# Summing a block's edges in the expert stage: one product of 195 columns and a reduction on VectorE in place of three products of 65

## The chip, the core and the metric

The kernel runs on one core of a Trainium2 chip. The metric is the device time of one execution in microseconds; lower is better. The five engines that the text names are TensorE (PE in the rows, its weight loads PEld), VectorE (DVE), ScalarE (ACT), GpSimd (POOL) and SyncE (SP).

## What is computed

Two graph layers over 6250 nodes with 256 features. The part that matters here is the first graph convolution and the mixture of eight experts that follows it:

```python
# first layer, graph part
x = features * norm_src @ W_gcn            # 64 columns a node
agg = segment_sum(x[src], dst)             # 106250 edges
h = relu(agg * norm_dst + b_gcn) @ W_out + b_out
# then, on the normalised sum of x, h and an attention term
w = softmax(feat @ Wr + br)                # 8 experts
y = relu(bn(feat @ W1[e] + b1)); y = relu(bn(y @ W2[e] + b2)); y = y @ Wo[e] + bo
x = x + sum_e w[e] * y[e]
```

A second attention layer on the same graph and a second mixture with a router graph follow; the change does not touch them.

## The kernel before

**Edges.** Edges are sorted by destination and cut into blocks of 128 that each belong to one window of 128 nodes. Four blocks (GROUP) make a group. For each block GpSimd gathers 128 rows of a table in DRAM by an indirect DMA (line 1455). A row holds the 64 features and a one (65 columns, GCOL) as three bfloat16 parts (PARTS) that add up to the float32 value, 195 columns in a row. VectorE builds a one-hot matrix of the four blocks' destinations (`one_hot`, line 1776). TensorE multiplies it with the rows (`edges`, lines 1470 to 1480): for each block three products of 65 columns add up in one region of PSUM. VectorE then adds each block's 65 columns to its window's sums in SBUF (`add_edges`, line 1791), each addition waiting for the one before, as two blocks can have the same window.

**Buffers.** `pe` has two PSUM banks, one for even and one for odd groups. Before group q TensorE waits until group q-2 has been added (line 1475). There are five buffers of gathered rows (ROWS) and three one-hot matrices (HOTS); both come free by the count of multiplied groups, `s_sum`.

**The expert stage.** The 49 windows go through in 7 chunks of 7 windows, and each chunk goes through 8 experts: 56 units (c, e). Within a unit TensorE, in a fixed order written out by hand, does the second layer of the expert in four quarters (`layer`, line 1566, l = 1), the first layer of the next expert (l = 0), and the last layer in four pairs of windows (`last`, line 1579). VectorE takes each last product, weighs it with the gate and adds it to the result (`weighted`, line 1895). ScalarE applies the activation after each layer (line 1704). The units' other work on VectorE is a piece of the router's sort (`sort.vector`, lines 1170 to 1232), in five of the eight experts of each chunk (e = 1 to 5). Experts 0, 6 and 7 have little or no sorting; 6 and 7 prepare the next chunk.

**Where edges lie in a unit.** 187 groups are spread over units 0 to 45, mostly four in a unit, in chunk 0 five or six. `share(unit, k)` names the groups of quarter k. On TensorE they come: share 0 ahead of `layer` l = 1, share 1 behind it, share 2 behind the next expert's `layer` l = 0, share 3 between the second and the third `last`. On VectorE: share 0 first, then the sort's piece 0, share 1, piece 1, share 2, piece 2, two `weighted`, piece 3 (line 1963), share 3 (line 1956), two `weighted`. Ahead of each group VectorE loads four window numbers into registers. Every engine takes its instructions in order, so an instruction that waits holds up all that stand behind it on its engine.

Of the kernel before, what the change touches and what calls it, by code (L numbers as in the profile page):

```python
# [10 lines left out]
ALU = mybir.AluOpType  # L11
ACT = mybir.ActivationFunctionType
AXX = mybir.AxisListType.X
ENG = mybir.EngineType

P = 128
# [15 lines left out]
PARTS = 3  # L32
GCOL = GCN + 1
# [18 lines left out]
GROUP = 4  # L52
# [206 lines left out]
class Prelude:  # L259
# [6 lines left out]
    ROWS = 6  # L266
    HOTS = 3
    KCB = 3
# [3 lines left out]
    VCOL = P + 1  # L272
    PAIRS = HALFKV // P
    KROW = HALFKV + PAIRS * VCOL

# [10 lines left out]
    def __init__(self, f, nc, R, A):  # L286
# [12 lines left out]
        self.rows = f.sb("rows", [P, self.ROWS, GROUP, GPAD], BF16)  # L299
        self.hot = f.sb("hot", [P, self.HOTS, P, GROUP], BF16)  # L300
        self.count = f.sb("count", [P, P, GROUP], BF16)
# [81 lines left out]
    def tensor(self, t):  # L383
        R = self.R

        def edges(q):
# [5 lines left out]
            for u in range(GROUP):  # L392
                for k in range(PARTS):
                    mm = t.matmul(self.pe[:, q % 2, u * GCOL:(u + 1) * GCOL], self.hot[:, q % self.HOTS, :, u],
                                  self.rows[:, b, u, k * GCOL:(k + 1) * GCOL], start=(k == 0), stop=(k == PARTS - 1))
# [65 lines left out]
    def vector(self, v):  # L461
# [4 lines left out]
        def one_hot(q):  # L466
            if q >= self.GROUPS:
                return
            if q >= self.HOTS:
                v.wait_ge(self.s_sum, q - self.HOTS + 1)  # L470
            v.tensor_tensor(self.hot[:, q % self.HOTS], self.count[:, :, :],
                            R.gdst[:, GROUP * q:GROUP * (q + 1)].unsqueeze(1).to_broadcast([P, P, GROUP]),
# [73 lines left out]
class Front:  # L546
# [3 lines left out]
    HALVES = GB // BAT  # L550
# [694 lines left out]
class Stage1:  # L1245
# [7 lines left out]

    ROWS = 5
    HOTS = 3
    PAIRS = -(-TPI // 2)
    UNITS = ITER * E0

# [68 lines left out]
    def __init__(self, f, nc, R, A):  # L1327
        self.nc, self.R, self.A = nc, R, A
        self.GROUPS = self.need(ITER - 1)
        self.acc = R.gacc  # L1330
        PAIRS = self.PAIRS
        store = R.XT[:, :, :].rearrange("p c n -> p (c n)")
        size = E0 * C * D

        def weights(k):
            return store[:, k * size:(k + 1) * size].rearrange("p (e c d) -> p e c d", e=E0, c=C)

        self.w1, self.w2, self.wo = (weights(k) for k in range(3))
        self.mw2 = R.ahead.mw2
        self.wout = R.ahead.wout  # L1340
        self.b2 = R.ahead.b2
        self.bg = R.ahead.bg
        self.wr = R.ahead.wr
        self.br = R.ahead.br
        self.bo, self.bop = R.ahead.bo, R.ahead.bop
        self.gs = f.sb("gs", [P, TPI, PARTS * 32])
        self.gb = f.sb("gb", [P, TPI, E0], BF16)
        self.bn = R.ahead.bn
        self.scale = f.sb("scale", [P, 2, E0 * C])
        self.shift = f.sb("shift", [P, 2, E0 * C])  # L1350
        self.rows = f.sb("rows", [P, self.ROWS, GROUP, GPAD], BF16)
        self.hot = f.sb("hot", [P, self.HOTS, P, GROUP], BF16)
        self.count = f.sb("count", [P, P, GROUP], BF16)
        self.xm = R.ahead.xm
        self.hid = f.sb("hid", [P, C, TOK])
        self.hf = f.sb("hf", [P, TPI, GCOL])
        self.nd = f.sb("nd", [P, TPI])
        self.ht = f.sb("ht", [GCOL, TPI, P])
        self.stats = f.sb("stats", [P, TPI, 6])
        self.mv = f.sb("mv", [P, TPI, 2])  # L1360
        self.var = f.sb("var", [P, TPI])
        self.std = f.sb("std", [P, TPI])
        self.rstd = f.sb("rstd", [P, TPI])
        self.xn = f.sb("xn", [P, TPI, D])
        self.xt = f.sb("xt", [P, C, TOK])
        self.lg = f.sb("lg", [P, TPI, E0])
        self.mx = f.sb("mx", [P, TPI])
        self.gate = f.sb("gate", [P, 2, TPI, E0])
        self.gt = f.sb("gt", [PARTS * 32, TPI, P], BF16)
        self.h1 = f.sb("h1", [P, C, TOK])  # L1370
        self.h2 = f.sb("h2", [P, C, TOK])
        self.pe = f.ps("pe", [P, 2, 512])
        self.ph = f.ps("ph", [P, 3, 512])
        self.po = f.ps("po", [P, 2, 2, D])
        self.side = f.ps("side", [P, 512])
        self.s_w = [f.sem(f"w{e}") for e in range(E0)]
        self.s_st, self.s_bn, self.s_bnr, self.s_scaled, self.s_made, self.s_cnt = (
            f.sem(n) for n in ("st", "bn", "bnr", "scaled", "made", "cnt"))
        self.s_rows = [f.sem(f"rows{b}") for b in range(self.ROWS)]
        self.s_hot, self.s_sum, self.s_acc = (f.sem(n) for n in ("hot", "sum", "acc"))  # L1380
        self.s_xm, self.s_mixed, self.s_side, self.s_sa, self.s_x = (
            f.sem(n) for n in ("xm", "mixed", "side", "sa", "x"))
        self.s_hf, self.s_nd, self.s_ndr, self.s_hr = (f.sem(n) for n in ("hf", "nd", "ndr", "hr"))
        self.s_bs, self.s_mv, self.s_var, self.s_std, self.s_xn = (f.sem(n) for n in ("bs", "mv", "var", "std", "xn"))
        self.s_lr, self.s_lg, self.s_ex, self.s_gate, self.s_total = (
            f.sem(n) for n in ("lr", "lg", "ex", "gate", "total"))
        self.s_h, self.s_g, self.s_o, self.s_a = (f.sem(n) for n in ("h", "g", "o", "a"))
        self.sort = RouterSort(f, nc, R, A)
        self.at = {u: k for k, u in enumerate(self.uses())}
        self.free, acts = [], 0  # L1390
        for what, n, k in self.uses():
            if what == "y":
                self.free.append((self.s_x, 2 * TPI * n + min(2 * k + 2, TPI)))
            elif what == "bo":
                self.free.append((self.s_x, 2 * TPI * n + TPI + min(2 * k + 2, TPI)))
            elif what == "lg":
                self.free.append((self.s_lr, n + 1))
            elif what == "sum":
                self.free.append((self.s_total, 1))
            else:  # L1400
                acts += 1
                self.free.append((self.s_sa, acts))
# [44 lines left out]
    def pool(self, g):  # L1447
        self.sort.pool(g)
        for q in range(self.GROUPS):
            b = q % self.ROWS  # L1450
            if q >= self.ROWS:
                g.wait_ge(self.s_sum, q - self.ROWS + 1)
            for u in range(GROUP):
                t = GROUP * (self.first() + q) + u
                g.indirect_dma_start(self.rows[:, b, u, :], None, self.R.tab0,  # L1455
                                     bass.IndirectOffsetOnAxis(self.R.gsrc[:, t:t + 1], 0)).then_inc(self.s_rows[b], 16)
# [3 lines left out]
    def tensor(self, t):  # L1460
# [9 lines left out]
        def edges(q):  # L1470
            b = q % self.ROWS
            t.wait_ge(self.s_hot, q + 1)
            t.wait_ge(self.s_rows[b], 16 * GROUP * (q // self.ROWS + 1))
            if q >= 2:
                t.wait_ge(self.s_acc, GROUP * (q - 1))
            for u in range(GROUP):
                for k in range(PARTS):
                    mm = t.matmul(self.pe[:, q % 2, u * GCOL:(u + 1) * GCOL], self.hot[:, q % self.HOTS, :, u],  # L1478
                                  self.rows[:, b, u, k * GCOL:(k + 1) * GCOL], start=(k == 0), stop=(k == PARTS - 1))
            mm.then_inc(self.s_sum, 1)  # L1480

        def mix(n, q):
            take("mix", n, q)
# [271 lines left out]
    def vector(self, v):  # L1755
# [13 lines left out]
        def one_hot(q):  # L1769
            if q >= self.GROUPS:  # L1770
                return
            if q >= self.HOTS:
                v.wait_ge(self.s_sum, q - self.HOTS + 1)
            t = GROUP * (self.first() + q)
            dst = R.gdst[:, t:t + GROUP]
            v.tensor_tensor(self.hot[:, q % self.HOTS], self.count[:, :, :],
                            dst.unsqueeze(1).to_broadcast([P, P, GROUP]), ALU.is_equal).then_inc(self.s_hot, 1)

        def add_edges(qs):
            for q in qs:  # L1780
                t = GROUP * (self.first() + q)
                _, ws = self.nc.values_load_multi_w_load_instructions(
                    R.gwin[0:1, t:t + GROUP], engines=(ENG.DVE,), min_val=0, max_val=W - 1,
                    skip_runtime_bounds_check_because="a count of at most W - 1 windows")
                aws = placed(v, columns_of(self.acc, ws))
                one_hot(q + self.HOTS - 1)
                v.wait_ge(self.s_sum, q + 1)
                for u, aw in enumerate(aws):
                    if GROUP * q + u:
                        v.wait_ge(self.s_acc, GROUP * q + u)  # L1790
                    v.tensor_tensor(aw, aw, self.pe[:, q % 2, u * GCOL:(u + 1) * GCOL], ALU.add).then_inc(self.s_acc, 1)  # L1791

        def gather_sums(n, done):
            win[n] = self.windows(ENG.DVE, n)
# [1850 lines left out]
```

## Time and profile before

| | us |
|---|---|
| median of 3 runs | 4489.13 (4483.42 to 4490.09) |
| profiled execution | 4484.99 |
| its span | 4483.3 |
| TensorE busy | 3576.9 (80%) |
| VectorE busy | 3140.5 (70%) |
| GpSimd busy | 2788.0 (62%) |
| ScalarE busy | 2405.0 (54%) |

The span is the time from the first to the last instruction of the profiled execution; the execution's own time is a little longer. A share of busy time over the whole span averages stages with different limits, so a stage is read from windows of its own. The last edge products of this stage start at 1567.91 us.

### The profile page before, as it was taken

The page shows a single profiled execution, that of the slowest core. Times are in us where ns is not written, and L with a number is a line of the kernel's source. Part 1 is how long each engine was busy: PE and PEld are TensorE (multiplying, and loading weights), DVE is VectorE, ACT ScalarE, POOL GpSimd, SP SyncE. Part 2 cuts the span into 40 slices and gives each one's busy share as a digit, 9 for nine tenths or more (in the row PEclk, how much of TensorE's full clock was granted, in tenths as well). Part 3 has the DMA queues.
Part 4 walks back from the last instruction along what each step waited for, and adds up shares of the span by engine and source line. Part 5 has one row for each costly group of instructions (what it writes and reads, how often), then busy time and mean ns, then how long its engine had stood idle before and what let it go on. Part 6 is the DMA issues. An engine that isn't in the chain of part 4 may idle for free. (4 is left out here: it accounts for less than half of the span.)

```text
span 4483.3 us, 67252 instructions
## 1 busy us (share of the span) xinstructions
PE 3576.9 (80%) x17779; PEld 2293.6 (51%) x17779; DVE 3140.5 (70%) x10032; ACT 2405.0 (54%) x5559; POOL 2788.0 (62%) x2880
## 2 busy tenths in 40 slices
PE   6697889999999998678878778855277777777763
PEld 6654556666666665444444445534144444444442
DVE  7676566565655654788888888875567777777777
ACT  7243223333233333489999974434466666666664
POOL 0175577676665400377777777764777777777774
PEclk9998999999999999899999999975589989898986
DMA  3233122121221101555555555534222222222221
GB/s 100 69 95 107 38 48 47 34 46 34 44 43 30 31 1 37 158 138 145 144 143 142 143 151 161 159 94 117 33 40 40 40 39 41 39 40 39 40 39 28
DMA packets 291737, 331.29 MB, mean 74 GB/s; under 512 B 80182, under 2 KB 246062, under 8 KB 291366
## 3 DMA queue, kind: packets, MB, share of 16 engines
q0 software_dynamic: 105328, 175.77, 19.2%
q1 hardware_dynamic: 186038, 151.23, 12.4%
q8 instruction: 153, 2.51, 0.2%
q14 instruction: 218, 1.79, 0.1%
HBM read 289.56 MB, written 30.77 MB: 71 GB/s over the span
## 5 line engine op out<-in xcount | busy, mean ns | idle before, releaser
L3108 POOL DMA_INDIRECT st_rows<-tabr,router_rsrc x1072 | 1030.3, 961 | 329.8 <-issue 317.0
L2438 POOL DMA_INDIRECT all_XT<-tab,graph_gsrc x880 | 843.7, 959 | 268.1 <-issue 233.3
L1455 POOL DMA_INDIRECT st_rows<-tab,graph_gsrc x748 | 733.1, 980 | 393.2 <-issue 205.1
L1704 ACT ACTIVATE st_h<-st_ph,st_shift,st_scale 128x448 f32<-128x448 f32 x448 | 323.9, 723 | 744.6 <-PE st_ph L1566 744.3
L2468 PE MATMUL st_po<-all_XT,st_hot 128*128 128x264 f32 x1760 | 517.7, 441 | 108.2 <-DVE gat_sum L2678 105.4
L3165 PE MATMUL st_py<-st_w,st_hid 128*128 128x256 f32 x1568 | 440.9, 430 | 2.8 <-ACT st_hid L3213 2.8
L2468 PEld LDWEIGHTS st_po<-all_XT,st_hot 128*128 128x128 f32 x1760 | 300.3, 202 | 249.1 <-issue 114.3
L2678 DVE TENSOR_TENSOR gat_sum<-gat_sum,st_po 128x264 f32 x880 | 375.8, 427 | 70.9 <-PE st_po L2468 1.7
L3153 PE MATMUL st_px<-all_XT,st_w 128*128 128x512 f32 (+2 forms) x832 | 390.8, 616 | 14.8 <-ACT st_hid L3213 14.8
L3127 PE MATMUL st_pad<-st_adr,st_hott 128*128 x1072 | 68.0, 175 | 405.5 <-DVE st_zd L3279 393.0
L1579 PE MATMUL st_po<-all_XT,st_h 128*128 128x256 f32 x1568 | 371.0, 385 | 8.5 <-DVE all_X L1895 6.7
L1566 PE MATMUL st_ph<-st_xt,all_XT 128*128 128x448 f32 x896 | 357.0, 550 | 0.0
L1566 PE MATMUL st_ph<-st_h,all_XT 128*128 128x448 f32 x896 | 355.8, 544 | 0.0
L3165 PEld LDWEIGHTS st_py<-st_w,st_hid 128*128 128x128 f32 x1568 | 315.8, 212 | 50.8 <-ACT st_hid L3213 3.1
L3202 ACT ACTIVATE st_rows<-st_d 128x16 f32<-128x16 f32 x268 | 57.9, 216 | 516.1 <-DVE st_d L3289 508.5
L1579 PEld LDWEIGHTS st_po<-all_XT,st_h 128*128 128x128 f32 x1568 | 290.6, 191 | 58.5 <-issue 14.5
L3127 PEld LDWEIGHTS st_pad<-st_adr,st_hott 128*128 128x128 bf16 x1072 | 51.6, 98 | 494.4 <-issue 464.6
L1791 DVE TENSOR_TENSOR gcn_acc<-gcn_acc,st_pe 128x65 f32 x748 | 165.8, 222 | 197.8 <-PE st_pe L1478 173.7
L2655 DVE TENSOR_TENSOR all_XT<-all_XT,st_wps 128x1024 f32<-128x1024 f32 x220 | 267.3, 1215 | 0.5 <-ACT all_XT L2574 0.5
L1895 DVE SCALAR_TENSOR_TENSOR all_X<-st_po,st_gate,all_X 128x256 f32 x392 | 169.4, 478 | 124.9 <-PE st_po L1579 122.7
L3314 DVE TENSOR_TENSOR router_racc<-router_racc,st_po 128x60 f32 x1072 | 229.8, 214 | 27.5
L3153 PEld LDWEIGHTS st_px<-all_XT,st_w 128*128 128x128 f32 x832 | 162.6, 206 | 169.0 <-issue 143.2
(519 smaller groups left out, 7337.2 us busy)
## 6 DMA issues: line engine op xcount, KB each, us to landing
st_bc<-drowr SPq DMA_DIRECT2D x268, 128.0 KB
st_bc<-drow SPq DMA_DIRECT2D x220, 128.0 KB
st_rows<-tabr,router_rsrc POOLq DMA_INDIRECT x1072
all_XT<-tab,graph_gsrc POOLq DMA_INDIRECT x880
st_xtb<-xtd SPq DMA_DIRECT2D x98, 128.0 KB
st_rows<-tab,graph_gsrc POOLq DMA_INDIRECT x748
tab<-gat_sum SPq DMA_DIRECT2D x7, 924.0 KB
xtd<-all_XT SPq DMA_DIRECT2D x49, 128.0 KB, 1.7
```

The costliest lines, as they stand in the source:

```text
L1455: g.indirect_dma_start(self.rows[:, b, u, :], None, self.R.tab0, bass.IndirectOffsetOnAxis(self.R.gsrc[:, t:t + 1], 0)).then_inc(self.s_ro ...
L1566: mm = t.matmul(self.ph[:, m % 3, 0:HALF], (self.w1, self.w2)[l][:, e, i, fb * P:(fb + 1) * P], src[:, i, h * HALF:(h + 1) * HALF], start= ...
L1579: mm = t.matmul(self.po[:, q % 2, j - 2 * k, :], self.h2[:, i, j * P:(j + 1) * P], self.wo[:, e, i, :], start=(i == 0), stop=(i == C - 1))
L1704: a.activation((self.h1, self.h2)[l][:, fb, h * HALF:(h + 1) * HALF], self.ph[:, m % 3, 0:HALF], ACT.Relu, bias=self.shift[:, l, i:i + 1], ...
L2438: g.indirect_dma_start(self.rows[:, b, u, :], None, self.R.tab1, bass.IndirectOffsetOnAxis(self.R.gsrc[:, t:t + 1], 0)).then_inc(self.s_ro ...
L2468: t.matmul(self.po[:, m % self.BANKS, 0:GROW], self.hot[:, q % self.HOTF, u], self.rows[:, q % self.ROWS, u, :], start=True, stop=True).th ...
L2655: v.tensor_tensor(m, m, self.wps[:, :, :].unsqueeze(3).to_broadcast([P, GROUP, GH, GC]), ALU.mult)\
L2678: v.tensor_tensor(aw, aw, self.po[:, (GROUP * q + u) % self.BANKS, 0:GROW], ALU.add).then_inc(self.s_acc, 1)
L3108: g.indirect_dma_start(self.rows[:, b, u, :], None, self.R.tabr, bass.IndirectOffsetOnAxis(self.R.rsrc[:, t:t + 1], 0)).then_inc(self.s_ro ...
L3153: mm = t.matmul(self.px[:, i, 0:n * P], self.w1[:, e, c, fb * P:(fb + 1) * P], R.XT[:, c, r * P:(r + n) * P], start=(c == 0), stop=(c == C ...
L3165: t.matmul(self.py[:, m % 2, 0:D], self.hid[:, (E1 * u + e) % 2, fb, j * P:(j + 1) * P], self.w2[:, e, fb, :], start=(fb == 0), stop=False)
L3314: v.tensor_tensor(aw, aw, self.po[:, q % self.SUMB, u * n:(u + 1) * n], ALU.add).then_inc(self.s_acc, 1)
```

## The change

Each block's edges become one product of 195 columns, which writes the three parts side by side to PSUM. Two blocks fill 390 columns of a bank, so a group takes both banks, a half (HALVES) in each. VectorE sums the three parts of a half with one reduction from PSUM into a new SBUF buffer `part` (new semaphore `s_part`), and the additions to the windows' sums read that buffer. TensorE's wait changes: a half of group q may be written when the same half of group q-1 has been reduced. `s_sum` now counts halves, and the waits on it are scaled. VectorE waits, ahead of each reduction, for the half's products and until the previous group's additions have read that half of `part`.

```diff
+    HALVES = 2
...
+        self.per, self.wide = GROUP // self.HALVES, PARTS * GCOL
...
+        self.part = f.sb("part", [P, self.HALVES, GROUP // self.HALVES, GCOL])
+        self.s_part = f.sem("part")
...
-                g.wait_ge(self.s_sum, q - self.ROWS + 1)
+                g.wait_ge(self.s_sum, self.HALVES * (q - self.ROWS + 1))
...
-            if q >= 2:
-                t.wait_ge(self.s_acc, GROUP * (q - 1))
-            for u in range(GROUP):
-                for k in range(PARTS):
-                    mm = t.matmul(self.pe[:, q % 2, u * GCOL:(u + 1) * GCOL], self.hot[:, q % self.HOTS, :, u],
-                                  self.rows[:, b, u, k * GCOL:(k + 1) * GCOL], start=(k == 0), stop=(k == PARTS - 1))
-            mm.then_inc(self.s_sum, 1)
+            for h in range(self.HALVES):
+                if q:
+                    t.wait_ge(self.s_part, self.HALVES * (q - 1) + h + 1)
+                for k in range(self.per):
+                    u = self.per * h + k
+                    mm = t.matmul(self.pe[:, h, k * self.wide:(k + 1) * self.wide], self.hot[:, q % self.HOTS, :, u],
+                                  self.rows[:, b, u, 0:self.wide], start=True, stop=True)
+                mm.then_inc(self.s_sum, 1)
...
-                v.wait_ge(self.s_sum, q - self.HOTS + 1)
+                v.wait_ge(self.s_sum, self.HALVES * (q - self.HOTS + 1))
...
-                v.wait_ge(self.s_sum, q + 1)
+                for h in range(self.HALVES):
+                    v.wait_ge(self.s_sum, self.HALVES * q + h + 1)
+                    if q:
+                        v.wait_ge(self.s_acc, GROUP * (q - 1) + self.per * (h + 1))
+                    v.tensor_reduce(self.part[:, h], self.pe[:, h, 0:self.per * self.wide]
+                                    .rearrange("p (u k c) -> p u c k", k=PARTS, c=GCOL), AXX, ALU.add)\
+                        .then_inc(self.s_part, 1)
                 for u, aw in enumerate(aws):
+                    v.wait_ge(self.s_part, self.HALVES * q + u // self.per + 1)
                     if GROUP * q + u:
                         v.wait_ge(self.s_acc, GROUP * q + u)
-                    v.tensor_tensor(aw, aw, self.pe[:, q % 2, u * GCOL:(u + 1) * GCOL], ALU.add).then_inc(self.s_acc, 1)
+                    v.tensor_tensor(aw, aw, self.part[:, u // self.per, u % self.per], ALU.add).then_inc(self.s_acc, 1)
```

## Rows read from the trace of the kernel before

**Rows 1.** Windows: engine busy us (instructions); clock, DMA share, GB/s at the end.

```profile
480.00:1580.00 1100.00, 1073.22 (x5780) 710.88 (x5779) 670.22 (x1951) 349.05 (x504) 714.06 (x728) 0.99 0.19 39
529.13:554.58 25.45, 22.78 (x144) 14.62 (x141) 21.58 (x57) 6.43 (x9) 19.35 (x21) 1.00 0.19 38
```

**Rows 2.** Groups by line, 480 to 1580 us: busy us, mean ns, idle before.

```profile
L1791 DVE TENSOR_TENSOR gcn_acc<-gcn_acc,st_pe 128x65 f32 x748 | 165.8, 222 | 197.8 <-PE st_pe L1478 173.7 <-issue 4.7
...
L1478 PE MATMUL st_pe<-st_rows,st_hot 128*128 128x65 bf16 x2244 | 103.5, 197 | 13.9 <-DVE gcn_acc L1791 8.0 <-issue 5.0 <-DVE st_hot L1776 1.0
```

**Rows 3.** Waits, 480 to 1580 us: total us, times, longest us.

```profile
DVE gcn_acc L1791 <- PE st_pe L1478: 173.7, 66, 6.8
...
PE st_pe L1478 <- DVE gcn_acc L1791: 8.0, 3, 2.7
...
PE st_pe L1478 <- issue: 5.0, 1, 5.0
```

**Rows 4.** Groups by line and shape on VectorE, the whole span.

```profile
L2637 DVE TENSOR_REDUCE st_zd<-st_pad 128x64 f32<-128x192 f32 x220 | 77.7, 353 | 27.4 <-issue 26.1
L3279 DVE TENSOR_REDUCE st_zd<-st_pad 128x32 f32<-128x96 f32 x268 | 68.7, 256 | 113.4 <-issue 110.9 <-PE st_pad L3127 2.4
...
L489 DVE TENSOR_REDUCE pre_ssum<-all_XT 128x16 f32<-128x512 f32 x49 | 33.5, 684 | 20.4 <-ACT all_XT L444 20.3
```

**Rows 5.** Timeline of an expert's end: start us, us, instruction, idle before.

```profile
1001.03 0.57 PE L1478 MATMUL st_pe<-st_rows,st_hot 128*128 128x65 bf16 x12
1001.44 3.70 PE L1579 MATMUL st_po<-all_XT,st_h 128*128 128x256 f32 x16
1001.64 1.00 DVE L1791 TENSOR_TENSOR gcn_acc<-gcn_acc,st_pe 128x65 f32 x4 [5.03 <-PE st_pe L1478]
...
1004.97 0.56 PE L1478 MATMUL st_pe<-st_rows,st_hot 128*128 128x65 bf16 x12
1005.17 0.88 DVE L1895 SCALAR_TENSOR_TENSOR all_X<-st_po,st_gate,all_X 128x256 f32 x2 [0.42 <-PE st_po L1579]
1005.37 2.83 PE L1579 MATMUL st_po<-all_XT,st_h 128*128 128x256 f32 x12
1005.97 0.68 DVE L1170 TENSOR_TENSOR st_skey<-st_skey 128x512 f32<-128x512 f32 x1
...
1008.04 0.56 PE L1478 MATMUL st_pe<-st_rows,st_hot 128*128 128x65 bf16 x12
1008.44 4.00 PE L1566 MATMUL st_ph<-st_h,all_XT 128*128 128x448 f32 x10
1009.37 0.43 DVE L1776 TENSOR_TENSOR st_hot<-st_count,graph_gdst 128x512 bf16<-128x512 bf16 x1 [0.80 <-PE st_pe L1478]
1009.72 0.99 DVE L1791 TENSOR_TENSOR gcn_acc<-gcn_acc,st_pe 128x65 f32 x4
```

**Rows 6.** Timeline: first and last of nineteen such ends, chunks 1 to 4.

```profile
734.34 0.56 PE L1478 MATMUL st_pe<-st_rows,st_hot 128*128 128x65 bf16 x12
...
735.87 0.99 DVE L1791 TENSOR_TENSOR gcn_acc<-gcn_acc,st_pe 128x65 f32 x4
...
1365.19 0.56 PE L1478 MATMUL st_pe<-st_rows,st_hot 128*128 128x65 bf16 x12
...
1368.22 0.98 DVE L1791 TENSOR_TENSOR gcn_acc<-gcn_acc,st_pe 128x65 f32 x4
```

**Rows 7.** Timeline: two groups one behind the other, expert 7 of chunk 0.

```profile
671.46 0.96 PE L1478 MATMUL st_pe<-st_rows,st_hot 128*128 128x65 bf16 x24
672.06 1.00 DVE L1791 TENSOR_TENSOR gcn_acc<-gcn_acc,st_pe 128x65 f32 x4 [0.24 <-issue]
```

**Rows 8.** Windows behind three long waits of TensorE; clock follows the five engines.

```profile
580.46:583.87 3.41, 3.41 (x6) 1.54 (x5) 3.22 (x11) 0.72 (x1) 2.67 (x3) 0.50 0.21 44
605.35:611.00 5.65, 5.65 (x26) 3.14 (x27) 5.13 (x17) 1.91 (x3) 4.33 (x5) 1.00 0.22 43
629.30:635.07 5.77, 5.77 (x24) 4.63 (x25) 3.01 (x12) 0.00 (x0) 4.53 (x5) 0.50 0.22 44
```

## The prediction

> **What bounds the kernel now.** The kernel's chain of waits ends in a later stage and says nothing of this one, so I read the expert stage by itself. First the windows: while edges are summed, 480 to 1580 us, TensorE is busy 1073.22 of 1100 us at a granted clock of 0.99 of 2.4 GHz, VectorE 670.22, and no other engine is near [rows 1]. TensorE is the bound, and any time by which it stands still is added to the stage, since the next stage starts behind this one. Next the groups by line: the 2244 edge products are small (65 columns each), and 748 additions on VectorE take their sums [rows 2]. Last the waits: VectorE waits 173.7 us for edge products, and TensorE waits for VectorE's additions only three times, 8.0 us in all, and once 5.0 us for something else [rows 3]. So today TensorE runs ahead and VectorE follows, up to two groups late; the wait in line 1475 asks only for the group before the last. That distance is what the change touches.
>
> **Part 1, TensorE's products.** A group of four blocks is now 12 products; from the first to the next line's product 0.41 us pass at 1001.03 and 0.40 us at 1004.97 [rows 5], 33 ns a product. At 2.4 GHz 65 columns stream in 27 ns, which leaves 6 ns for each product. The change streams the same 12 x 65 = 4 x 195 = 780 columns in four products of 81 + 6 = 87 ns, 0.35 us: 0.05 us less, times 187 groups 9 us. Bounds: nothing if the whole cost goes by columns; 8 x 33 ns x 187 = 50 us if it goes wholly by products. I take 9, since 27 of 33 ns are columns at the granted clock.
> The Trainium skill (TensorE: Matmul & The Clock Gate, Back-to-back issue gap) gives 81 ns for each pair of weight load and product at 128 columns in a sustained stream. By that, as an estimate from the page, dropping eight pairs of twelve would give back some 0.6 us a group and the time would come out near 4520; the row's 33 ns a pair speaks against it.
>
> **Part 2, VectorE's work.** Each group gets two reductions of 128x390 to 128x130. The same form (three strided parts, out of PSUM) runs in other stages: 256 ns for 96 elements, 353 ns for 192; 512 elements from SBUF take 684 ns [rows 4]. The first two give 1.01 ns an element, so 390 cost 353 + 198 x 1.01 = 553 ns. Bounds: 353 and 684 ns; I take 553, since the line through all three rows runs there. Two a group are 1.11 us, 374 in all 207 us. The four additions read SBUF in place of PSUM; at 65 columns I leave them at 222 ns [rows 2]. The added waits on VectorE (for sums already made, for parts already added) are met when it gets there. VectorE's idle time in the stage is 430 us, so by busy time alone this would be hidden. It is not, because of its order.
>
> **Part 3, the new wait on TensorE.** Both banks now hold halves of one group, so group q may be multiplied only when group q-1 has been reduced; before, q-2 had to be added. Behind that wait stand, in TensorE's one queue, the 16 products of the next layer, and behind those ScalarE's activations. VectorE's queue places the fourth additions of an expert behind the sort's last piece (the piece is issued at k = 1, line 1963, the additions at k = 2, line 1956), while TensorE goes from the fourth edges through the last two `last` steps (12 products) straight into the next expert's first edges. Walk one such end. TensorE starts the fourth edges at 1004.97 and the next expert's at 1008.04, but VectorE starts the fourth additions at 1009.72 [rows 5]: it is 1.67 us late already, and nobody minded. After the change:
> - the third edges' sums come at 1001.64 after 5.03 us of idle [rows 5]; two reductions push what follows by 1.11 us. The pause of 0.42 us ahead of 1005.17 takes some of it, so the sort's piece of 1005.97 and the fourth sums come 0.7 us later, at 1010.42;
> - their two reductions take until 1011.5; TensorE's half products then end near 1011.8, where now they end at 1008.44 [rows 5].
> TensorE loses 3.4 us: the old lateness of 1.67 plus 1.7. By the third edges VectorE has caught up (it idles 5.03 us there now), so the loss is not made good and not doubled: it comes once for each expert.
>
> Now the sum, over the five sorting experts of each chunk. In chunks 1 to 4 there are 19 ends where an expert with sorting passes to one with first edges. The old lateness at them (start of group q-1's first addition less start of group q's first product) runs from 735.87 - 734.34 = 1.53 at the first to 1368.22 - 1365.19 = 3.03 at the last, as low as 0.20 [rows 6]; the 19 sum to 41.7 us. With 19 x 1.7 = 32 that is 74 us. In chunk 5 two such ends (1.64 and 4.71) give 10. In chunk 0 five sorting experts have 27 groups, often two in a row; there VectorE already fills the period (21.58 us of 25.45, much of the rest its register loads) [rows 1], so its added 27 x 1.11 = 30 us show, less some 5 of idle it can eat: 25. Pairs of groups one behind the other outside the sorting experts (six): the second group starts 0.40 us behind the first, whose sums VectorE takes at 672.06, 0.60 after 671.46 [rows 7]; with 1.11 of reductions that is 1.3 to 1.4 us each, 9 in all with small change. Sum of waits: 74 + 10 + 25 + 9 = 118 us. Less Part 1: 109.
>
> **Part 4, the clock.** TensorE's four long waits of today are 8.0 / 3 = 2.7 us each and one of 5.0 [rows 3]. After one of the three the granted clock fell to 1.2 GHz for 3.41 us; after another it stayed at 2.4; after the one of 5.0 us 5.77 us ran at 1.2 [rows 8]. The third of the three was not followed by a fall either. Work at 1.2 GHz loses half: 0, 0, 1.7 and 2.9 us, 1.15 on average. Some 26 new waits of 2 to 6 us lie in the like range; bounds 0 and 26 x 2.9 = 75 us. I take 1.0 each, 26 us, as a few of the new waits are shorter than today's four.
>
> **Sum.** 109 + 26 = 135 us more. The profiled execution took 4484.99 us with a span of 4483.3, 4 us under the median of 4489.13; the difference goes onto the median: 4624 us. A measurement of this kernel tells about 0.2%, 9 us, from no change.
>
> **The rivals.**
> - *The clock falls after nearly every wait.* TensorE now stands still at each expert's end, so a stretch at 1.2 GHz follows each. For it: the longest wait of today was followed by the longest such stretch [rows 8]; against it: two of four had none. 26 x 2.9 = 75 us in place of 26 gives 4673, with reductions at their upper bound (684 ns, some 20 us more) 4693. The Trainium skill (TensorE: Matmul & The Clock Gate, Why this matters for your kernels) advises to leave no idle gaps between bursts of matmuls, as the clock falls back in them; the trace agrees for two of the four.
> - *Only the old lateness is paid.* If the reductions fall into VectorE's pauses (idle of 5.03 us and less before the third sums [rows 5]), an end costs the old lateness and little more: 48 us for 21 ends, 15 in chunk 0, 6 for the pairs, no fall of the clock, less 9: 60 us, 4549. Against it: the fourth group's own two reductions have no pause in front of them.
> - *TensorE stays the bound and nothing is late* (the other side). Mechanism: TensorE's first short wait moves it behind VectorE once and for all, and from then on each group is reduced before TensorE returns; place, the expert's end; it decides from the point where VectorE has reduced the fourth sums within the 3.07 us from 1004.97 to 1008.04 [rows 5]. Then only Part 1 is left: 9 us, at most 50, 4480 to 4439. Against it: VectorE idles 5.03 us before each third sum, so its lateness is made anew inside every expert by the sort's pieces.
> - *VectorE becomes the bound throughout.* If reductions out of PSUM with a stride cost more than the rows say, VectorE's order sets every period: 207 us and the clock on top, above 4705.
>
> **How the numbers follow.** Forecast (4580 to 4660) 0.55; clock after nearly every wait 0.20; only the old lateness 0.17; TensorE stays the bound 0.04; VectorE the bound throughout 0.04. Range 4545 to 4705, which takes in the first three and leaves out the last two and their like. Faster by over 0.2%: 0.03; within 0.2%: 0.02; slower: 0.95.
>
> **What would show it.** In the profile after: 748 edge products, about 0.35 us a group; 374 reductions near 553 ns on VectorE; TensorE waiting for these reductions some 30 to 45 times, 100 us or more in all, in place of 8.0; unit lengths longer by 3 to 5 us where sorting runs and unchanged after the last edges at 1568 us; stretches at a granted clock of 0.5 behind the waits. I would be wrong if TensorE's busy share of the stage stays at 97%, if VectorE's fourth additions come before TensorE's next first edges, or if the edge products' own time drops by more than 0.1 us a group.

## The result, and the profile after

The changed kernel takes 4632.44 us (4628.37 to 4634.05), 1.0328 times the kernel before, interval 1.0315 to 1.034: 145 us slower than the runs of the kernel before that go with it (median 4487.0 us). The forecast was 4624 us, range 4545 to 4705. The profiled execution has a span of 4632.1 us.

The windows of the stretch in which edges are summed, now 480 to 1720 us (busy us of TensorE, weight loads, VectorE, ScalarE and GpSimd, then the granted clock, DMA share, GB/s):

```profile
480.00:1720.00 1240.00, 1104.45 (x4273) 707.42 (x4272) 845.71 (x2315) 345.67 (x499) 717.92 (x728) 0.95 0.17 34
```

Beside [rows 1]: TensorE stood still for 27 us of 1100, now for 136 of 1240, and its mean granted clock fell from 0.99 to 0.95 of 2.4 GHz. Units 46 and later, which have no edges, take nearly what they took (18.29 us each for the experts 1 to 3 of chunk 6, before and after). Of the 149 us between the spans of the two profiled executions, 144 lie in units 0 to 45, where edges are.

The groups by line of the same stretch, the edge products and the new reductions:

```profile
L1483 PE MATMUL st_pe<-st_rows,st_hot 128*128 128x195 bf16 x748 | 104.6, 258 | 101.5 <-DVE st_part L1796 100.7
...
L1796 DVE TENSOR_REDUCE st_part<-st_pe 128x130 f32<-128x390 f32 x374 | 192.4, 556 | 150.2 <-PE st_pe L1483 150.0
L1803 DVE TENSOR_TENSOR gcn_acc<-gcn_acc,st_part 128x65 f32 x748 | 169.0, 226 | 60.9 <-DVE gcn_acc L1803 3.4
```

And TensorE's waits for VectorE (total us, times, longest us), first the two kinds at other lines as the kernel before had them, then the changed kernel's:

```profile
PE st_po L1579 <- DVE all_X L1895: 6.7, 8, 2.0
...
PE st_side L1519 <- DVE st_xn L1841: 3.1, 5, 0.6
```

```profile
PE st_pe L1483 <- DVE st_part L1796: 100.7, 34, 8.2
...
PE st_po L1584 <- DVE all_X L1907: 16.8, 13, 2.9
...
PE st_side L1524 <- DVE st_xn L1853: 14.4, 8, 2.3
```

Three waits of 8.0 us in [rows 3] became 34 of 100.7. The same expert's end as in [rows 5], on the timeline:

```profile
1070.79 0.50 PE L1483 MATMUL st_pe<-st_rows,st_hot 128*128 128x195 bf16 x4
1071.13 3.64 PE L1584 MATMUL st_po<-all_XT,st_h 128*128 128x256 f32 x16
1071.16 1.03 DVE L1796 TENSOR_REDUCE st_part<-st_pe 128x130 f32<-128x390 f32 x2 [3.76 <-PE st_pe L1483]
1072.11 1.29 DVE L1803 TENSOR_TENSOR gcn_acc<-gcn_acc,st_part 128x65 f32 x4
...
1074.61 0.50 PE L1483 MATMUL st_pe<-st_rows,st_hot 128*128 128x195 bf16 x4
...
1075.57 2.86 PE L1584 MATMUL st_po<-all_XT,st_h 128*128 128x256 f32 x12 [0.46 <-DVE all_X L1907]
1076.22 0.68 DVE L1170 TENSOR_TENSOR st_skey<-st_skey 128x512 f32<-128x512 f32 x1
...
1079.96 1.03 DVE L1796 TENSOR_REDUCE st_part<-st_pe 128x130 f32<-128x390 f32 x2
1080.67 0.74 PE L1483 MATMUL st_pe<-st_rows,st_hot 128*128 128x195 bf16 x4 [2.24 <-DVE st_part L1796]
```

The reader sees the walk of the prediction: the fourth edges are multiplied at 1074.61, their reductions stand behind the sort's piece and start at 1079.96, and TensorE, ready 2.24 us earlier, starts the next expert at 1080.67, when the first half has been reduced.

### The profile page after: what moved, and what is told of

Read it like the earlier page. It is cut to its first block and busy times, and to the rows that moved or that the text cites. A ratio compares the mean times of both kernels' runs of the same rounds, so it can differ in the third digit from the quotient of the medians.

```text
span 4632.1 us, 65567 instructions
## 1 busy us (share of the span) xinstructions
PE 3633.0 (78%) x16283; PEld 2308.0 (50%) x16283; DVE 3318.3 (72%) x10406; ACT 2404.7 (52%) x5559; POOL 2792.2 (60%) x2880
## 5 line engine op out<-in xcount | busy, mean ns | idle before, releaser
L1584 PE MATMUL st_po<-all_XT,st_h 128*128 128x256 f32 x1568 | 378.9, 391 | 18.7 <-DVE all_X L1907 16.8
L1571 PE MATMUL st_ph<-st_h,all_XT 128*128 128x448 f32 x896 | 378.8, 573 | 0.0
L1796 DVE TENSOR_REDUCE st_part<-st_pe 128x130 f32<-128x390 f32 x374 | 192.4, 556 | 150.2 <-PE st_pe L1483 150.0
L1571 PEld LDWEIGHTS st_ph<-st_h,all_XT 128*128 128x128 f32 x896 | 178.1, 204 | 152.2 <-issue 137.0
```

The costliest lines, as they stand in the source:

```text
L1571: mm = t.matmul(self.ph[:, m % 3, 0:HALF], (self.w1, self.w2)[l][:, e, i, fb * P:(fb + 1) * P], src[:, i, h * HALF:(h + 1) * HALF], start= ...
L1584: mm = t.matmul(self.po[:, q % 2, j - 2 * k, :], self.h2[:, i, j * P:(j + 1) * P], self.wo[:, e, i, :], start=(i == 0), stop=(i == C - 1))
```

## The experiments

Times stand beside runs of the kernel before on the same chip: 4484.41 us for the first four, 4483.29 for the last four.

| kernel | us | ratio (interval) | against before |
|---|---|---|---|
| wait_only | 4615.54 | 1.0294 (1.0276 to 1.0311) | +131 |
| load_only | 4563.46 | 1.0174 (1.0157 to 1.0191) | +79 |
| early_after | 4557.80 | 1.0163 (1.0147 to 1.0180) | +73 |
| early_before | 4486.01 | 1.0007 (0.9998 to 1.0017) | +2 |
| product_only | 4472.80 | 0.9980 (0.9971 to 0.9989) | -10 |
| early_wait | 4499.76 | 1.0036 (1.0023 to 1.0049) | +16 |
| load_one | 4503.81 | 1.0043 (1.0028 to 1.0059) | +21 |
| early_load | 4544.42 | 1.0132 (1.0117 to 1.0148) | +61 |

**wait_only.** The distance of one group alone, in the kernel before:

```diff
-            if q >= 2:
-                t.wait_ge(self.s_acc, GROUP * (q - 1))
+            if q >= 1:
+                t.wait_ge(self.s_acc, GROUP * q)
```

> The kernel before with the shorter distance alone: TensorE starts a group when the group before it has been added (not the one before the last); twelve products of 65 columns and no reduction. The theory of the prediction, that TensorE waits at the end of a sorting expert for sums that VectorE's queue places behind a piece of the sort: most of the 145 us appear without any added work on VectorE. An end costs the old lateness and the fourth additions themselves (1.0 us in place of 1.7): 48 + 21 us at 21 ends, 15 in chunk 0, 7 for pairs, and about 30 for the clock: 4590 to 4620 us. The rival, that the 207 us of added work on VectorE are the cause: within 20 us of the kernel before.

Measured: 131 us more, near the upper end of what the wait theory allowed, without one added instruction on VectorE. TensorE's wait for edges has the same count as in the changed kernel:

```profile
PE st_pe L1478 <- DVE gcn_acc L1791: 107.2, 34, 6.6
```

The rival that the added work alone is the cause falls.

**load_only.** Two reductions a group on VectorE, on constant data, the old distance:

```diff
+                for h in range(2):
+                    if q:
+                        v.wait_ge(self.s_part, 2 * q + h - 1)
+                    v.tensor_reduce(self.part[:, h], self.mw2[:, :, :].rearrange("p c d -> p (c d)")[:, 0:6 * GCOL]
+                                    .rearrange("p (u k c) -> p u c k", k=PARTS, c=GCOL), AXX, ALU.add)\
+                        .then_inc(self.s_part, 1)
```

> The kernel before with the two reductions for each group on VectorE (128x390 to 128x130, here from constant data in SBUF, the result is not used) and the old distance of two groups. Theory: TensorE's old wait is rarely reached, so only chunk 0, where VectorE fills the period, pays: 15 to 45 us, 4500 to 4535. Rival, VectorE's work as the bound: 100 us or more, over 4585.

Measured: 79 us more, between the two theories, and a miss for mine (15 to 45). The reductions from SBUF were 593 ns, a little dearer than the 556 ns out of PSUM. Its waits of TensorE show where the load is paid, and it is mostly not at the edges (13.9 us of idle there before, [rows 2]):

```profile
L1793 DVE TENSOR_REDUCE st_part<-ahead_mw 128x130 f32<-128x390 f32 x374 | 206.1, 593 | 115.6 <-PE st_pe L1480 115.4
```

```profile
PE st_po L1581 <- DVE all_X L1903: 33.9, 19, 4.3
PE st_pe L1480 <- DVE gcn_acc L1799: 15.8, 7, 4.2
PE st_side L1521 <- DVE st_xn L1849: 15.5, 6, 3.0
```

The first wait (st_po) is at the last layer, whose two buffers VectorE frees by `weighted`; the third (st_side) is in expert 7, where VectorE's normalised rows come later. The unit of expert 7 grew by 5.3, 3.5, 3.8, 5.0 and 5.0 us in chunks 0 to 4.

**early_after and early_before.** One move on VectorE: the fourth additions (and reductions) ahead of the sort's last piece, in the changed kernel and in the kernel before:

```diff
                     if k == 2:
-                        add_edges(self.share(unit, 3))
+                        if su is None:
+                            add_edges(self.share(unit, 3))
...
                     if k == 1 and su is not None:
+                        add_edges(self.share(unit, 3))
                         self.sort.vector(v, sst, su, 3)
```

> The changed kernel with one move on VectorE: in a sorting expert the fourth group's reductions and additions stand ahead of the sort's last piece instead of behind it. Theory: the 21 ends lose their wait (74 + 10 us) and the falls of the clock behind them (30 to 40 us), chunk 0 and the pairs keep theirs: 4510 to 4560 us. Rival, VectorE's work as the bound: the move changes no work, so within 15 us of 4632.

> The same move in the kernel before, as the control. Theory: with a distance of two groups nobody waits for the fourth additions except in chunk 0 (8.0 us in three waits), so 0 to 15 us faster than the kernel before, 4472 to 4489. Rival, that the move is worth something by itself (for instance by letting the sort run beside other work): over 30 us faster.

Measured: the move gives the changed kernel 75 us back (4632 to 4558; the theory's upper end was 4560) and the kernel before nothing (+2, with an interval of the ratio that takes in 1). The waits for reductions shrink from 34 to 19, those of expert 7 stay, and those of the last layer grow from 16.8 to 25.4 us:

```profile
PE st_pe L1483 <- DVE st_part L1796: 35.6, 19, 6.4
PE st_po L1584 <- DVE all_X L1907: 25.4, 16, 4.8
PE st_side L1524 <- DVE st_xn L1853: 15.7, 9, 2.3
```

With no added work, the place of the fourth additions matters only with the distance of one group, as the walk said. The remaining 73 us are left for the load; early_load, below, tests that.

**early_wait and early_load.** The same move in wait_only and in load_only.

```diff
                     if k == 1 and su is not None:
+                        add_edges(self.share(unit, 3))
                         self.sort.vector(v, sst, su, 3)
```

> The shorter distance alone, with the fourth additions ahead of the sort's last piece. Theory, by what the first runs showed (131 us for the distance, 80 for the added work, 148 for both, and the move gives back 75): the ends vanish, chunk 0 and the pairs stay, 15 + 7 us of waits and some 10 of the clock: 4500 to 4530. If the distance costs wherever the additions stand, it stays over 4580.

> The two unused reductions for each group with the old distance, and the fourth additions ahead of the sort's last piece. Theory: what the added work costs (79 us) falls on waits of the last layer's products, on the experts that prepare the next chunk and on chunk 0, and none of these is at the fourth additions, so it stays within 15 us of 4563. If it falls to under 4520, the place of the fourth additions is the cause of the added work's cost too.

Measured: with the move the distance costs 16 us in place of 131 (4499.76, at the lower edge of what was expected); the load still costs 61 in place of 79 (4 us below the band I gave), so the move gives back 18 us of the load's cost too. TensorE's waits for edges in early_wait:

```profile
PE st_pe L1478 <- DVE gcn_acc L1791: 25.8, 14, 4.7
```

So the four corners read: with the additions behind the sort, distance 131, load 79, both together with the products 145 to 148; with the additions ahead of it, distance 16, load 61, both 73. The parts do not add up behind the sort. A likely reason is that VectorE catches up with its load while TensorE waits at an expert's end; the smaller waits of the last layer in the changed kernel (16.8 us, 33.9 in load_only) agree, but no run tests it by itself. The load of load_only is also not quite that of the change: its reductions read SBUF, and its additions keep their old pace (see Part 2 below).

**load_one.** One unused reduction a group in place of two (`for h in range(1)`).

> The kernel before with one reduction for each group on VectorE in place of two (result not used), old distance. Theory: VectorE has some idle time in most experts, so the first half of the work costs less than half of the 79 us of two: 10 to 35 us, 4495 to 4520. If every added us on VectorE cost alike, 40 us, 4524.

Measured: 21 us for the first 187 reductions (one a group), 58 more for the second 187 of load_only (79 - 21). The cost is not proportional to the work; that VectorE's idle time covers part of the first ones is the expectation's account, which this agrees with.

**product_only.** The products alone:

```diff
-                for k in range(PARTS):
-                    mm = t.matmul(self.pe[:, q % 2, u * GCOL:(u + 1) * GCOL], self.hot[:, q % self.HOTS, :, u],
-                                  self.rows[:, b, u, k * GCOL:(k + 1) * GCOL], start=(k == 0), stop=(k == PARTS - 1))
+                mm = t.matmul(self.pe[:, q % 2, u * GCOL:(u + PARTS) * GCOL], self.hot[:, q % self.HOTS, :, u],
+                              self.rows[:, b, u, 0:PARTS * GCOL], start=True, stop=True)
```

> The kernel before with the products alone changed: four of 195 columns in place of twelve of 65, written into the old places of the old two banks, each overwriting what its neighbour left beyond 65 columns. The additions then take the first of the three parts only: the sum of the parts is left out. Old distance, no reduction. Theory: 0.05 us a group, 9 us, 4472 to 4480 us. Rival, that a product's cost goes by columns alone: no change.

Measured: 10 us less, as expected to a microsecond or two. This is what the wider products gave where the sum of the parts costs nothing. No version found here beats the kernel before with the parts summed: early_after is the best of the changed kernel, 73 us behind.

## Why the prediction was right, and where its terms were off

The direction, the mechanism and the sum held: 145 us against 135. Its steps:

- **Part 1, products (forecast 9 us gained).** Held by product_only, 10 us. From the first product to the next line's 0.34 us pass now (1070.79 to 1071.13), 0.40 before [rows 5]. A second gain was not in the prediction: the next line's products pass faster too, 16 in 3.64 us where [rows 5] has 3.70, so a unit without sorting (expert 0 of chunk 2) fell from 22.13 to 21.76 us, 0.09 us a group or 17 us for 187. So the gain a group was nearly twice the forecast, and the 10 us of product_only match the forecast in part by luck: its profiled execution has nine stretches at 1.2 GHz with 33 us of running products, where the kernel before has four with 19, and 2 us more of idle time.
- **Part 2, reductions (forecast 553 ns).** 556 ns. The additions were taken as unchanged and the added waits on VectorE as costing nothing. Each addition is 226 ns, but four of them now take 1.21 us (median of 187 groups; 1.29 in the end shown) where they took 0.99. The pause between two of them is 104 ns in place of 34, although the reductions had ended: all but the first of a group now stand behind two waits, not one. Reading SBUF does not explain it, since other chained VectorE steps of the changed kernel that read SBUF behind one wait (lines 1821 to 1824) still have pauses of 34 to 35 ns. That is 0.2 us a group, 45 us in all, more on VectorE than the sum has.
- **Part 3, waits (forecast 118 us).** TensorE's idle time in units 0 to 45 rose from 26.8 to 135.6 us: 109. By parts, from the timeline: the 19 ends 53.6 us at the edges, plus 10 more in waits of the last layer, against 74; the two ends of chunk 5 7 against 10; chunk 0 24 more against 25. The end that the prediction walked shows 2.24 + 0.46 = 2.7 us of idle time; by starts, from the fourth edges to the next expert's first 6.06 us pass (1074.61 to 1080.67) where 3.07 did (1004.97 to 1008.04), 2.99 us more, not 3.4. Two things in the timeline make it less: VectorE starts on the first half 0.37 us after TensorE's first product (1071.16), not 0.6, and TensorE starts again after the first half's reduction, not after both. Five pairs cost 0.62 us each at the edges, not 1.3 to 1.4, for the same reason. Not foreseen were 11 us in expert 7, at the transposes of the next chunk's rows (14.4 against 3.1): the prediction looked for the price of the load at the edges only, and load_only shows that it falls on other waits. Nor was a second, short stop: behind a wait the third product of a group waits again, for the other half's reduction. At 1080.67 the four products take 0.74 us, not 0.50; over the 19 such waits at 2.4 GHz the extra is 0.24 us each, in wait_only nothing. For all 34 that is an estimated 8 us, which the idle time does not count.
- **Part 4, clock (forecast 26 us).** The term that was too small. Mean clock 0.95 over 1240 us means some 124 us at 1.2 GHz, and there are 26 such stretches in units 0 to 45 where there were 4. Counted over the clock's records, 105 us of them fall on running products, 19 before; half of the difference, 43 us, is lost. Of the 26 stretches, 23 begin during a wait of 2.0 to 8.2 us or within 1.6 us of its end; the other three begin in or behind a row of 28 products of eight columns with no wait right ahead, as two of the four before do. By windows, first at one end in the changed kernel, then at such a row in the kernel before:

```profile
1486.38:1489.94 3.56, 0.00 (x1) 0.03 (x2) 2.74 (x6) 0.00 (x0) 1.02 (x1) 0.90 0.14 28
1489.94:1496.07 6.13, 6.13 (x12) 3.00 (x13) 5.07 (x17) 0.72 (x1) 3.78 (x4) 0.50 0.13 27
```

```profile
1246.06:1252.89 6.83, 6.83 (x14) 3.60 (x14) 1.07 (x4) 0.72 (x1) 0.52 (x1) 0.50 0.08 16
```

TensorE stands still for 3.56 us and then needs 6.13 us at 1.2 GHz for 12 products; in such stretches a product of 448 columns starts 0.747 us after the last, where at 2.4 GHz it is 0.376. The prediction priced the new falls by four waits, of which two were followed by one; that was too small a sample, and 1.0 us each became 43 / 26 = 1.7.

Balance: 109 of waits, 8 of second stops and 43 of clock, less 17 for the products, is 143 of the stage's 144. For wait_only the same count, 86 of waits and 43 of clock, gives 129 of 131.

Of the rivals, the clock after nearly every wait was half true (23 falls behind the 43 waits of over 1 us); that only the old lateness is paid is refuted (109 us of waits against 69 of its sum without the products); that TensorE stays the bound with nothing late is refuted by 34 waits. VectorE as the bound throughout is not what happens (it is busy 846 of 1240 us), but load_only shows that the load by itself costs 79 us, more than the 15 to 45 expected of it.

That the sum came out close owes something to luck, as errors of opposite sign met in it: the clock cost 17 us more than forecast and the products gave 8 us more. The waits with the second stops, 117 us against 118, agree for the same reason: the ends and pairs were priced too high, and expert 7 and the second stops were not in the sum.

## What to carry to other kernels

Buffers shared by two engines set how far one may run ahead: here a change that halved that distance turned the lateness of the second engine into waits of the first, although the second engine had 430 us of idle time. Before such a change, list at each use how late the second engine is today (its start less the first engine's next start); expect to pay what is positive, and what stands between in the second engine's queue can sometimes be moved. An engine that is busy 61% of a stage is also not free to load: one added reduction a group cost 21 us, the second 58. And count the waits that an edit adds to a chain of short instructions: each one here cost its engine 70 ns, though already met.

## What the runs showed of the hardware

- The granted clock's fall cost as much as 40% of the waits themselves (43 us beside 109). It came with waits of 2.0 to 8.2 us (23 of 26 stretches), and in both kernels also with rows of 28 products of eight columns with no wait right ahead (three stretches after the change, two before).
- Between two chained additions on VectorE 34 ns passed with one wait and 104 ns with two, the second already met (561 pauses of each).
- A train of 12 short products with weight loads also delays the products behind it: the first step of the next line was 0.296 us with 12 and 0.241 with 4, where a step within the line is 0.216 (256 columns, expert 0 of chunk 2, from the single records of the trace). Four in place of 12 gave about as much there (0.055 us) as in the train itself (0.399 to 0.344). In product_only the same 0.241 is found. What holds the next line's load was not tried.
- Reductions of 390 elements with stride took 556 ns out of PSUM and 593 ns from SBUF.
